# A two-layer Mamba, expert and windowed-attention kernel on one core: the end projection of layer 1 cut into four pieces and moved from slot 6 to slots 19 to 22, the eighth scan step moved to slot 7, and two elementwise steps on GpSimd

## The reference

```
x = hidden                                    # 8 x 512 x 128
xn = layernorm(x)
x = x + mamba(xn) + top1_experts(xn)          # layer 0
xn = layernorm(x)
x = x + window_attention(xn) + gated_ffn(xn)  # layer 1

mamba: hs, gate = split(xn @ in_proj.T); u = silu(conv4(hs))
       dt, B, C = rmsnorms(u @ x_proj.T); dt = softplus(dt @ dt_proj.T + b)
       h[t] = exp(dt[t] A) h[t-1] + dt[t] u[t] B[t]         # 256 channels x 16 states
       y = (sum over states of h C + u D) * silu(gate) @ out_proj.T
window_attention: 16 heads of 8, |i-j| <= 32; softmax(q k / sqrt(8) + mask) v @ Wo + bo
gated_ffn: (silu(xn wg) * (xn wu)) @ wd
```

## Time and profile before

| | |
|---|---|
| median of three runs | 1037.47 us |
| the profiled execution's own time | 1045.25 us |
| its span, first to last instruction | 1043.5 us |
| PE busy | 822.6 us, 79% |
| DVE busy | 721.7 us, 69% |
| ACT busy | 654.0 us, 63% |
| POOL busy | 509.9 us, 49% |
| mean granted TensorE clock | 0.902 of full speed |
| chain that ended last, by engine | PE 39%, DVE 19%, ACT 17%, issue 11%, POOL 10%, DMA 3% |

### The profile page before, as it was taken

The page is one execution under the profiler, slowest core; times in us unless marked ns, Lnnn a source line. Parts: engine busy times, 40 slices in busy tenths (PEclk is TensorE's granted clock), DMA queues, the critical chain, the costliest instruction groups (busy, mean ns, idle before and its releaser), DMA issues.

```text
span 1043.5 us, 15599 instructions
## 1 busy us (share of the span) xinstructions
PE 822.6 (79%) x5226; PEld 565.1 (54%) x5226; DVE 721.7 (69%) x983; ACT 654.0 (63%) x1999; POOL 509.9 (49%) x293
## 2 busy tenths in 40 slices
PE   1854888784897889788978887888788877888685
PEld 0622887772654575456545654665466544654443
DVE  7759344357776977596768676867687758787475
ACT  0242566653697558756885688468845884596564
POOL 2367231516665466635663576357625862472100
PEclk9957899996898889889988998899889997899898
DMA  7464899884442444344434542354234423550000
GB/s 226 155 200 129 235 294 301 256 205 91 115 94 62 112 123 103 62 104 120 113 61 97 129 106 60 99 135 94 62 95 134 96 63 82 142 113 12 20 12 11
DMA packets 85952, 123.20 MB, mean 118 GB/s; under 512 B 8560, under 2 KB 43760, under 8 KB 85744
## 3 DMA queue, kind: packets, MB, share of 16 engines
q1 hardware_dynamic: 79584, 115.38, 42.6%
q0 software_dynamic: 6288, 6.82, 2.9%
HBM read 106.21 MB, written 12.29 MB: 114 GB/s over the span
## 4 chain that ended last, share of the span: by engine, by line
PE 39%; DVE 19%; ACT 17%; issue 11%; POOL 10%; DMA 3%; SPq 1%; DVEq 0%; POOLq 0%; ACTq 0%
DVE hst L813 6%; ACT pexp L1103 6%; PE y_bank L1319 5%; PE more L1451 5%; ACT dA L1025 4%; POOL xs_d L1173 3%; PE work L1338 2%; DVE dBu L805 2%; POOL hc L1205 2%; ACT pT L1116 2%; PE work_l L1463 2%; PE more L1463 2%; PE work L1364 1%; PE work L1297 1%; PE work_l L1290 1%
## 5 line engine op out<-in xcount | busy, mean ns | idle before, releaser
L1205 POOL TENSOR_TENSOR hc<-hst,bcr 128x1024 f32<-128x1024 f32 x116 | 277.4, 2392 | 344.1 <-DVE dBu L805 317.5
L813 DVE TENSOR_TENSOR_SCAN hst<-dA,dBu 128x1024 f32<-128x1024 f32 x128 | 291.8, 2279 | 6.3 <-ACT dA L1025 5.5
L1025 ACT ACTIVATE dA<-dt,neg_a 128x511 f32<-128x511 f32 x256 | 171.1, 727 | 28.3 <-DVE hst L813 25.7
L805 DVE TENSOR_TENSOR dBu<-dtu,bcr 128x1024 f32<-128x1024 f32 x128 | 161.8, 1264 | 28.0 <-DMA bcr<-bc_d 16.3
L1319 PE MATMUL y_bank<-pk,hc 128*128 128x128 f32 x1024 | 150.2, 294 | 14.1 <-POOL hc L1205 10.6
L1451 PE MATMUL more<-pk,pexp 128*96 128x128 f32 x480 | 109.0, 298 | 59.4 <-ACT pexp L1103 53.9
L1319 PEld LDWEIGHTS y_bank<-pk,hc 128*128 128x128 f32 x1024 | 127.8, 152 | 50.7 <-issue 26.9
L1451 PEld LDWEIGHTS more<-pk,pexp 128*96 128x96 f32 x480 | 58.0, 127 | 108.4 <-issue 49.2
L950 DVE TENSOR_REDUCE nmax<-work 128x4 f32<-128x384 f32 x60 | 33.3, 556 | 82.3 <-PE work L1372 65.7
L1116 ACT COPY pT<-more 96x512 f32<-96x512 f32 x120 | 70.0, 583 | 29.5 <-PE more L1451 29.2
L1103 ACT ACTIVATE pexp<-work_l,nmax 128x96 f32<-128x96 f32 x240 | 78.7, 348 | 14.3 <-DVE nmax L950 14.2
(11 more groups left out here) (375 smaller groups left out, 1572.2 us busy)
## 6 DMA issues: line engine op xcount, KB each, us to landing
bcr<-bc_d SPq DMA_DIRECT2D x128, 512.0 KB, 5.2
qbd<-in_wx SPq DMA_DIRECT2D x8, 578.0 KB, 5.0
o_all<-in_wx SPq DMA_DIRECT2D x8, 578.0 KB, 5.2
pT<-in_wx SPq DMA_DIRECT2D x8, 578.0 KB, 5.1
kT<-in_wx SPq DMA_DIRECT2D x8, 578.0 KB, 4.8
vw<-in_wx SPq DMA_DIRECT2D x8, 578.0 KB, 5.0
xs_d<-rbuf POOLq DMA_DIRECT2D x1, 2560.0 KB, 9.7
hst<-in_hidden SPq DMA_DIRECT2D x8, 256.0 KB, 6.7
```

The lines of the kernel that those rows point to most:

```text
L805: v.tensor_tensor(dBu[:], dtu[par], bcr[n % RING][:, 0:1, :].to_broadcast([P, NH, L]), ALU.mult).then_inc(s_dBu, 1)
L813: v.tensor_tensor_scan(hst[n % 2][:].rearrange("p h t -> p (h t)"), dA[n % 2][:].rearrange("p h t -> p (h t)"), dBu[:].rearrange("p h t -> ...
L1025: s.activation(dA[n % 2][:, h, 1:L], dt[par][:, h, 1:L], ACT.Exp, scale=neg_a[:, h, n:n + 1]).then_inc(s_dA, 1)
L1205: g_.tensor_tensor(hc[n % 2][:], hst[n % 2][:], bcr[n % RING][:, 1:2, :].to_broadcast([P, NH, L]), ALU.mult).then_inc(s_hc, 1)
```

## The change

- `STEP_AT`: scan step 7 goes from slot 8 to slot 7, step 14 from slot 23 to slot 22. `MID`: `ss` goes from slot 8 to slot 7.
- The end projection `fin` becomes four units, one for each block of 128 tokens: in slots 19, 20, 21 and 22. Piece 0 holds the bias matmul and the wait for `attnT`. `y_out` goes to slot 23, `avg` to slot 17.
- `fin` takes the bank of layer 0, `work[0]` (bank 5 of the list), in place of `more`. It waits for that bank's last reader of the turn (`dtp1`), and the next turn's first user (`xnT`) waits until `y_out` has read it.
- The bias of `attnT` is added on POOL behind `avg`, in place of ACT.
- `ln_set` goes from slot 18 to 19, `dln` from slot 19 to 20.
- SP's moves of heads go from the spreads of steps 0 to 3 to those of steps 4 to 7 (`HEADS_AT`); `kin` in slot 4 is now ahead of them.
- In the last turn the same units stand in the table `LAST_AT`, the four pieces one behind the other.

```diff
-STEP_AT = (0, 1, 2, 3, 4, 5, 6, 8, 10, 12, 14, 16, 18, 20, 23, 25)
+STEP_AT = (0, 1, 2, 3, 4, 5, 6, 7, 10, 12, 14, 16, 18, 20, 22, 25)
-MID = {3: [("scan", "slots", 0)], 8: [("pre", "ss", 0)], 25: [("pre", "dtu", 0)]}
+MID = {3: [("scan", "slots", 0)], 7: [("pre", "ss", 0)], 25: [("pre", "dtu", 0)]}
...
-        5: [("pre", "xdbl", 0), ("finish", "avg", 0), ("attn", "v2", 0)],
-        6: [("finish", "fin", 0), ("finish", "attnT", 0), ("attn", "v3", 0)],
-        7: [("finish", "y_out", 0)],
+        5: [("pre", "xdbl", 0), ("attn", "v2", 0)],
+        6: [("attn", "v3", 0)],
...
-        18: [("pre", "de", 0), ("pre", "ln_set", 0)], 19: [("pre", "dw", 0), ("pre", "dln", 0)], 21: [("pre", "dt", 0)],
+        18: [("pre", "de", 0)], 19: [("pre", "dw", 0), ("pre", "ln_set", 0), ("finish", "fin", 0)],
+        20: [("pre", "dln", 0), ("finish", "fin", 1)], 21: [("pre", "dt", 0), ("finish", "fin", 2)],
+        22: [("finish", "fin", 3)], 23: [("finish", "y_out", 0)],
...
-                    if name == "spread" and k < RG and b >= 2:
-                        own_head_rows(b - 2, k)
-                        if k == RG - 1:
+                    if name == "spread" and HEADS_AT <= k < HEADS_AT + RG and b >= 2:
+                        own_head_rows(b - 2, k - HEADS_AT)
+                        if k == HEADS_AT + RG - 1:
                             averages_of(b - 2)
...
-                elif name == "attnT":
-                    act.wait_ge(s_avg, b + 1)
-                    done1(act, b, f"up{HC - 1}")
-                    s.activation(attnT[:], fth[:], ACT.Identity, bias=pc("bv")).then_inc(s_attnT, 1)
...
                         g_.tensor_tensor(fth[:], fth[:], rd_rows, ALU.mult).then_inc(s_avg, 1)
+                        pool.wait_ge(s_avg, b + 1)
+                        g_.tensor_scalar(attnT[:], fth[:], pc("bv"), None, ALU.add).then_inc(s_attnT, 1)
...
+                    if k == 0:
+                        take1_after(pe, b, name, *[f"up{c}" for c in range(HC)])
+                        ahead = b + LAG["finish"] - LAG["pre"]
+                        if ahead < B:
+                            done0(pe, ahead, "dtp1")
...
+                        pe.wait_ge(s_attnT, b + 1)
+                    q = slice(k * P, (k + 1) * P)
+                    for c in range(HC):
+                        t.matmul(w1k(b, name)[:, q], fh[:, c, q], ffn[:, 2, c * P:(c + 1) * P], start=False, stop=False)
+                    last = t.matmul(w1k(b, name)[:, q], attnT[:, q], pc("wo"), start=False, stop=(k == NT - 1))
```

More of the change, by code:

```diff
@@ L82 @@
         12: [("pre", "zg1", 0)], 13: [("pre", "sg1", 0), ("pre", "dtT", 0), ("scan", "rows", 2)],
-        15: [("pre", "dtp0", 0), ("scan", "rows", 3)], 17: [("pre", "dtp1", 0)],
-        18: [("pre", "de", 0), ("pre", "ln_set", 0)], 19: [("pre", "dw", 0), ("pre", "dln", 0)], 21: [("pre", "dt", 0)],
+        15: [("pre", "dtp0", 0), ("scan", "rows", 3)],
+        17: [("pre", "dtp1", 0), ("finish", "avg", 0)],
+        18: [("pre", "de", 0)], 19: [("pre", "dw", 0), ("pre", "ln_set", 0), ("finish", "fin", 0)],
+        20: [("pre", "dln", 0), ("finish", "fin", 1)], 21: [("pre", "dt", 0), ("finish", "fin", 2)],
+        22: [("finish", "fin", 3)], 23: [("finish", "y_out", 0)],
         24: [("attn", "fg", 0), ("attn", "fu", 0)],
@@ L90 @@
 SUM_LAG = 2
+HEADS_AT = 4
 O_LAST = 4
-LAST_AT = {0: [("v2", 0), ("v3", 0)], 3: [("avg", 0), ("attnT", 0)], 4: [("fin", 0), ("y_out", 0)], 6: [("fg", 0), ("fs", 0), ("fu", 0), ("fh", 0)], 8: [("fg", 1), ("fs", 1), ("fu", 1), ("fh", 1)], 10: [("fg", 2), ("fs", 2), ("fu", 2), ("fh", 2)],
+LAST_AT = {0: [("v2", 0), ("v3", 0)], 3: [("avg", 0)], 4: [*[("fin", j) for j in range(NT)], ("y_out", 0)], 6: [("fg", 0), ("fs", 0), ("fu", 0), ("fh", 0)], 8: [("fg", 1), ("fs", 1), ("fu", 1), ("fh", 1)], 10: [("fg", 2), ("fs", 2), ("fu", 2), ("fh", 2)],
            12: [("ffn_down", 0)], 13: [("proj", 0), ("proj", 1)],
@@ L204, in keys @@
 def keys(name, k):
-    if name in ("out", "q", "k", "v0", "v1", "v2", "v3", "rdT", "fin"):
+    if name in ("out", "q", "k", "v0", "v1", "v2", "v3", "rdT"):
         return [name]
-    return {"scores": [f"s{k}"], "turn": [f"pT{k}"], "fg": [f"gate{k}"], "fu": [f"up{k}"], "ln_b": ["xnT"], "yT": ["yT0", "yT1"],
+    return {"scores": [f"s{k}"], "turn": [f"pT{k}"], "fg": [f"gate{k}"], "fu": [f"up{k}"], "ln_b": ["xnT"], "fin": ["fin"] if k == NT - 1 else [], "yT": ["yT0", "yT1"],
             "values": ["oL" if k == G - 1 else "oK"], "proj": [f"fin{k}"] if k >= 2 else []}.get(name, [])
-L1_BANK = {"yT0": 1, "yT1": 2, "out": 0, "xnT": 1, "q": 0, "k": 1, "v0": 2, "v1": 0, "v2": 1, "v3": 0, "rdT": 2, "fin": 2,
+L1_BANK = {"yT0": 1, "yT1": 2, "out": 0, "xnT": 1, "q": 0, "k": 1, "v0": 2, "v1": 0, "v2": 1, "v3": 0, "rdT": 2, "fin": 5,
            **{f"s{k}": k % 2 for k in range(G)}, **{f"pT{k}": 2 for k in range(G)},
@@ L226, in l1_bank @@
         return LAST_BANK[key]
-    return 5 if (b, key) == (B - 2, "fin") else L1_BANK[key]
+    return L1_BANK[key]
 def l1_before(b, key, bank=None):
@@ L478, in take0 @@
             before(eng, s_free0, b * L0_N + L0_USES.index(key))
+            if key == "xnT":
+                done1(eng, b + LAG["pre"] - 1 - LAG["finish"], "fin")
         def done0(eng, b, key):
@@ L1488, in layer1 @@
                 elif name == "fin":
[L1489 to L1502 removed]
+                    if k == 0:
[3 more added lines that the diff above has]
+                            done0(pe, ahead, "dtp1")
+                        if b == 0:
+                            pe.wait_ge(s_bias, 9)
+                        t.matmul(w1k(b, name)[:].rearrange("p (j d) -> p j d", d=H), onesb[0:96, :],
+                                 bias_rows[:].unsqueeze(1).to_broadcast([96, NT, H]), start=True, stop=False)
+                        pe.wait_ge(s_attnT, b + 1)
[3 more added lines that the diff above has]
+                    last = t.matmul(w1k(b, name)[:, q], attnT[:, q], pc("wo"), start=False, stop=(k == NT - 1))
+                    if k == NT - 1:
+                        last.then_inc(s_full1, 1)
             def body(it, par):
```

15 lines of the change are left out of this document (1 added, 14 removed).

## The result

| | kernel before | changed kernel |
|---|---|---|
| median of four runs of each in one job | 1037.45 us (1035.1 to 1040.5) | 1024.87 us (1023.6 to 1028.1) |
| ratio, 95% interval | | 0.988 [0.985, 0.992] |
| profiled execution, its span | 1045.25, 1043.5 us | 1025.76, 1024.0 us |
| PE busy, share of the span | 822.6 us, 79% | 817.7 us, 80% |
| DVE busy | 721.7 us | 728.7 us |

The change is faster, by 12.6 us or 1.2%. A gain of 33 us and a time of 1004.5 us were forecast. The time is still inside the range of 994 to 1026, by one microsecond, but the forecast was wrong in the size of the gain. The executions of the kernel before spread from 1031 to 1046 us over all jobs, and both of its profiled executions (1045.25, 1045.53) lie at the upper end.

The account below looks back on a forecast made before the run. No engine fills a turn; waits on PE, across POOL and a low end clock bound it. Turns 2 to 6 gain 5 x (3.3 + 2.0), turn 1 2.0, turn 7 4.5: 33.0 us, less the 7.8 offset, 1004.5 us, range 994 to 1026.

Parts of the forecast that it names:

- the ring load's term: Head of the turn: a load for step 7 as late as before would cost 2.0 us of the head's gain.
- the crossing of POOL: Slots 8 to 10: chain from row sums through POOL's product and step 7's sum to ACT's copy; sum to copy 1.57 us.
- the clock at the end: Slots 24 and 25: low clock costs 3.0 us; filled PE gaps were to win back 2.0 us a turn.
- the head: Slots 5 to 11: `v3` no longer waits for the 3.79 us end projection; gain 3.3 us a turn.
- 0.7 was forecast: Slots 19 to 22: pieces delay the exp of group 15 by some 0.7 us; net cost taken as 0.
- turns 0 and 1: Turn 0, paced by the experts' tiles, gains 0; turn 1, without a finish, gains only 2.0 us at its end.
- the anchor: Whole kernel: the median was taken 7.8 us below the profiled execution, so 1012.25 became 1004.5 us.
- C: Head: the ring load lands no earlier than before and takes the wait; head gains 1.3 us, 1016.5 us; chance 0.11.
- D: Slots 19 to 22: pieces at 1.2 GHz take 7.6 us a turn, uncovered; slower, 1063 us; chance 0.08.
- E: POOL's crossing grows by what PE gives up and the end stays at 1.2 GHz: 1037 us; chance 0.05.
- B: End of the turn keeps 1.2 GHz, so only the head gains: 1018.5 us; chance 0.18.
- A: Clock stays high to the turn's end, 3.0 us in place of 2.0: 997 us; chance 0.22.

Follow-up runs that it names:

- the short filler: Changed kernel plus 4 matmuls with overwritten result in PE's wait ahead of the sum of step 7: 1009.9 us, ratio 0.971.
- the pieces alone: Changed kernel with scan steps 7 and 14 and the row sums back in slots 8, 23 and 8: 1019.8 us, ratio 0.979.
- the late sum: Changed kernel with the sum of step 7 in slot 10, behind the turn of group 1: 1004.9 us (0.966), again 1002.4 us (0.964).
- step 7 alone: Kernel before with only scan step 7 and `ss` moved to slot 7: 1027.9 us, ratio 0.987.
- step 7 moved and step 14 back: Changed kernel with scan step 14 back in slot 23: 1028.1 us, ratio 0.988.

## Why the prediction was wrong

**What held.** Scan 6, product, scan 7 without a wait; the ring load's term was 2.0 us, its wait came back as 1.81 and cost 1.4 a turn. Exp of group 0 starts 8.1 us behind scan 6 (forecast 8.2), that of group 1 10.4 (10.3), the sum of step 7 12.79 (12.8). POOL has room for the average and the bias: they end at 719.17, ahead of step 12's product at 720.72, and the bias takes 1.58 us, forecast 1.8:

```profile
716.22 1.26 POOL L1221 TENSOR_TENSOR fth<-fth,y_out 128x512 f32<-128x512 f32 x1
717.59 1.58 POOL L1223 TENSOR_SCALAR fsg<-fth,pk 128x512 f32<-128x512 f32 x1
720.72 2.36 POOL L1206 TENSOR_TENSOR hc<-hst,bcr 128x1024 f32<-128x1024 f32 x1 [1.55 <-DVE dBu L810]
```

**The step that failed** is the one from the sum of step 7 to ACT's copy, in the crossing of POOL: "From the sum to ACT's copy 1.57 us (708.54 - 706.97)". I took that stretch at full clock, from a row of the kernel before. It took 693.57 - 690.70 = 2.87 us, at 1.2 GHz; the sum alone takes 1.97 us in each of turns 2 to 6. So exp of group 3 came 19.6 us behind scan 6, not 18.3. Where the clock stays full, in turn 5 of the short filler, it comes 687.88 - 669.57 = 18.31 us behind, wait and all, which is the forecast. The prediction named the clock as a risk at the pieces and at the end of the turn, but not in the crossing. It also took 2.0 us a turn from the clock at the end without asking whether another stretch would fall: over the turn, the low clock stayed at some 17 us.

What the new wait did is less clear than its place suggests. It did not bring the fall, which comes 1.1 us ahead of it, and the pieces alone and some turns of the kernel before have a low stretch in the crossing without it. Filling it with matmuls ended the stretch sooner. What makes the clock fall there stays open.

**What it did to the rest of turn 5**, from starts on the timelines: the head gained 2.0 us in place of 3.3. From the exp of group 10 to that of group 15 it became 2.1 us longer (17.03 to 19.09), 0.7 was forecast. Part of that is the clock again, at 726 to 729, on the bias and piece 0 (the three groups take 0.63, 1.49 and 0.63 us, a piece at full clock 0.83 and 0.39), part a wait for the row maximum of group 15. Without the low clock this stretch is 17.73 us. The end, from that exp to the reciprocal, gained 2.4; 2.7 was in the sum (0.7 behind exp 15 and 2.0 of clock): half of its low stretch went, about as I took it, but with the short filler or the late sum all of it goes. Another 0.5 came between the exps of groups 3 and 10, and 0.6 ahead of scan 6, which I had at 0. Sum of turn 5: 2.0 + 0.5 - 2.1 + 2.4 + 0.6 = 3.4, as by the reciprocals, in place of 3.3 - 0.7 + 2.7 = 5.3.

**The account.** 33.0 forecast, 19.5 in the span: turns 2 to 6 fell short by 6.7 us (26.5 against 19.8), turns 0 and 1 by 5.1 (+2.0 against -3.1), turn 7 by 1.2, the last by 0.5. Of the 5.1, turn 0 has 2.2: the 16 matmuls that start the states' sums of turn 1 begin at 232.9 us in place of 230.7, where I had put 0. The cause isn't shown. They begin at 232.4 with step 7 alone and at 229.9 with the pieces alone, which speaks for the move of step 7 among the experts' tiles, but at 230.7 with step 7 moved and step 14 back, and the late sum has 232.2 and 233.1 in two executions of one program. The other 2.9 lie in turn 1; the late sum won them and more, the short filler only 0.7, which I have not followed up.

The remaining 6.9 us are the anchor. I took 7.8 us off the forecast because the profiled execution of before lay that far above the median. The changed kernel has no such offset, 0.9 (1025.76 against 1024.87). So of the 19.5 us between the two profiled executions the medians see 12.6. Long executions aren't peculiar to the profile: others of the kernel before took 1042 to 1046 us too, at the same low mean clock. Whether both profiled ones were such by chance, and why the same program has executions at 0.90 and at 0.916, stays open.

**The rivals.** C, ring load late, fell: no wait for a transfer. D fell: bias and piece 0 do run at 1.2 GHz, but the stretch of the pieces grew by only 2.1 us a turn. E fell by the turn's length. B is nearest in size (1018.5), with the wrong mechanism: the end did not keep the low clock whole. A comes near what the same kernel does with the short filler: turns of 99.06 us, 6.7 less than before, where A had 6.3 for turns 2 to 6. The rule cited with A, from the Trainium skill ("TensorE: Matmul & The Clock Gate", What's actually happening), is that activity releases the throttle. The traces agree in the direction that I didn't use: the clock falls at 688.0 behind 4 us with PE busy for 2.48, and with step 7 alone it falls at 695.9 behind 6 us with PE busy for 3.89; four added matmuls in the wait bring it back sooner. But the work just ahead doesn't settle it: in turn 5 of the short filler PE has the same gap (1.50 us) ahead of the same scores, and the clock doesn't fall.

**A better version.** The changed kernel with the sum of step 7 in slot 10 runs in 1002 to 1005 us in two jobs, some 3.5% under the kernel before and 2% under the changed one.

## What to carry to other kernels

When a change adds a wait on TensorE, price the wait, and price the work around it at half clock as well; look in the windows whether the work just ahead of it is already thin, and add up the low clock over the whole turn, not over the one stretch that the change is meant to mend. First try to put the waiting group behind work that is ready; here that brought 20 us. Where nothing is ready, a few matmuls into a free bank, shorter than the wait, can win clock back: 15 us here. When a filler is judged, look at every turn and not at one. And take a forecast's anchor from several executions of the kernel before, and look at their mean clock: an offset between the profiled execution and the median need not carry over to the changed kernel.
